# The second feed-forward product by seven products of quarter matrices instead of eight

## The reference

```python
xW = einsum('ntd,dh->nth', x, Wx) + b
next_h = tanh(xw_t + prev_h @ Wh)            # scan over 2048 steps, h0 = cond_1024
...
def quant_linear(x, w, b):
    xq, s_in = quant_act_uint8(x)             # one scale for the whole tensor: max / 255
    wq, s_w = quant_weight_int8_perchannel(w) # one scale per output row: max|w| / 127
    bq = quant_bias_int32(b, s_in, s_w)
    return einsum('btd,fd->btf', xq, wq) + bq
h = relu(quant_linear(rnn, w1, b1))
return x + quant_linear(h, w2, b2)
```

## Time and profile before

| what | value |
|---|---|
| three runs | 501.76, 502.87, 497.11 us |
| span of the profiled execution (first to last instruction) | 496.8 us |
| TensorE busy | 477.3 us, 96% |
| VectorE, ScalarE, GpSimd busy | 293.4, 235.6, 94.8 us |
| mean granted clock of TensorE | 0.997 |
| second product on the chain of waits | from 382.6 us on |
| bytes moved | 65.37 MB |

### The profile page before, as it was taken

How to read it: one execution, slowest core, us unless ns; L and a number is a source line. 1 busy time by engine, 2 the same in 40 slices (tenths; PEclk the granted TensorE clock), 3 DMA queues, 4 the chain that set the end, 5 groups by cost and what they waited for, 6 DMA issues and landing times.

```text
span 496.8 us, 8656 instructions
## 1 busy us (share of the span) xinstructions
PE 477.3 (96%) x3003; PEld 326.9 (66%) x3003; DVE 293.4 (59%) x476; ACT 235.6 (47%) x450; POOL 94.8 (19%) x69
## 2 busy tenths in 40 slices
PE   8989999999999999999767999999999999999997
PEld 3668888888999999999754444444443444444443
DVE  2797664468233354545678978878778433454442
ACT  0324544554333232323573888888884334343340
POOL 2840471210000000000000000000000554444355
PEclk9998999999999999999999999999999999999999
DMA  8974422110349000000000777200002089888883
GB/s 294 386 257 169 171 86 84 41 46 1 74 95 169 0 1 0 0 0 0 2 1 3 299 294 323 101 0 1 0 1 85 35 302 303 304 274 306 308 314 133
DMA packets 38165, 65.37 MB, mean 132 GB/s; under 512 B 19056, under 2 KB 19200, under 8 KB 34560
## 3 DMA queue, kind: packets, MB, share of 16 engines
q1 hardware_dynamic: 37472, 64.04, 37.4%
q10 hardware_dynamic: 576, 1.05, 0.6%
q0 software_dynamic: 96, 0.01, 0.0%
HBM read 39.93 MB, written 20.97 MB: 123 GB/s over the span
## 4 chain that ended last, share of the span: by engine, by line
PE 87%; DVE 7%; DMA 2%; ACT 1%; issue 1%; SPq 1%; DVEq 0%; ACTq 0%
PE bank L794 22%; PE bank L859 22%; PE bank L584 15%; PE bank L621 12%; PE bank L627 12%; PE bank L611 3%; DMA arena<-w 2%; DVE arena L1203 2%; PE bank L647 2%; DVE arena L1342 1%; DVE w_absmax L1196 1%; ACT arena L1059 1%; DVE arena L1562 0%; SPq L424 0%; DVE arena L1252 0%
## 5 line engine op out<-in xcount | busy, mean ns | idle before, releaser
L560 POOL TENSOR_SCALAR arena<-arena,bq 128x512 f32<-128x512 f32 x32 | 53.2, 1676 | 336.9 <-DVEq L1605 284.4
L794 PE MATMUL bank<-arena,w_words 128*128 128x512 f16 (+1 forms) x512 | 110.7, 379 | 0.7 <-DVE arena L1440 0.7
L859 PE MATMUL bank<-arena,w2t 128*128 128x512 f16 x512 | 110.7, 379 | 0.5 <-DVE arena L1568 0.5
L1098 ACT ACTIVATE arena<-bank,bq,s_bits 128x512 f32<-128x512 f32 x124 | 89.1, 774 | 27.3 <-PE bank L794 15.0
L859 PEld LDWEIGHTS bank<-arena,w2t 128*128 128x128 f16 x512 | 49.7, 98 | 61.5 <-DVE arena L1562 2.0
L794 PEld LDWEIGHTS bank<-arena,w_words 128*128 128x128 f16 x512 | 50.0, 98 | 61.0 <-DVE arena L1440 1.5
L1521 DVE TENSOR_REDUCE hid_parts<-arena 128x1 f32<-128x1024 f32 x60 | 72.2, 1216 | 20.4 <-ACT arena L1098 19.8
L621 PE MATMUL bank<-arena 128*128 x512 | 63.5, 277 | 0.1
L627 PE MATMUL bank<-arena 128*128 x512 | 62.4, 275 | 0.0
L621 PEld LDWEIGHTS bank<-arena 128*128 128x128 f32 x512 | 59.7, 192 | 0.7 <-issue 0.5
L627 PEld LDWEIGHTS bank<-arena 128*128 128x128 f32 x512 | 59.7, 192 | 0.0
(11 more groups left out here) (104 smaller groups left out, 354.9 us busy)
## 6 DMA issues: line engine op xcount, KB each, us to landing
spill<-arena SPq DMA_DIRECT2D x12, 1024.0 KB, 3.9
arena<-spill SPq DMA_DIRECT2D x12, 1024.0 KB, 8.4
arena<-w SPq DMA_DIRECT2D x8, 1024.0 KB, 5.2
arena<-x_t SPq DMA_DIRECT2D x32, 256.0 KB, 3.9
y_t<-arena SPq DMA_DIRECT2D x32, 256.0 KB, 2.1
arena<-x_t SPq DMA_DIRECT2D x7, 1024.0 KB, 8.8
arena<-x_t ACTq DMA_DIRECT2D x4, 256.0 KB, 5.7
arena<-wx SPq DMA_DIRECT2D x4, 256.0 KB, 5.4
```

The lines of the kernel that those rows point to most:

```text
L560: nc.gpsimd.tensor_scalar(xb[:, d], xb[:, d], bq2[:, d:d + 1], None, ALU.add).then_inc(xb_ready, 1)
L794: mm = nc.tensor.matmul(bank[:, f % 8, :], w1t[:, k, f * P:(f + 1) * P], states_in[:, k, :], start=(k == 0), stop=(k == KT - 1))
L859: return nc.tensor.matmul(bank[:, 4 + d, :], w2t[:, f, d * P:(d + 1) * P], hq[:, f % HQ_RING, :], start=(f == 0), stop=(f == FT - 1))
L1098: kept = nc.scalar.activation(out[:, e, :], bank[:, (f + e) % 8, :], ACT.Identity, bias=bq1[:, f + e:f + e + 1], scale=s1_bits[:, f + e:f ...
```

## The change

Group 4 goes first and keeps the plain product of 64 matmuls. The other seven follow in the order 0, 1, 2, 3, 5, 6, 7 (`ORDER`). For each of them the hidden values (2048 x 512) and w2 are cut into quarters, and the output's four quarters B00, B01, B10, B11 (halves of the 512 features by halves of the 512 tokens) come from seven products of quarter matrices. A product is 16 matmuls of 256 columns: 8 hidden tiles by 2 output tiles. Products 1, 6, 7 and 4 go into the same bank one upon the other, and between them ScalarE copies the partial result out (`keep_piece`), scaled and with the bias; GpSimd adds the copy to x (`add_piece`); VectorE adds what products 2, 5 and 3 left in the two other banks (`add_out`). VectorE makes four differences of hidden quarters per group (`hidden_sums`, 2048 float16 per partition each), GpSimd three and VectorE one of w2. The hidden integers of a whole group now stand in SBUF, in the first half of the place of their float32 values, two groups ahead.

x and the output lie in memory by groups and quarters, so a partition's part of a group is 8 KB in one piece. The first reload of x is issued right after the spills. The loops over the groups are written out. The waits of the last stage are new.

```diff
+ORDER = (LAST, 0, 1, 2, 3, 5, 6, 7)
+B00, B01, B10, B11 = range(4)
+FIRST_ACT, FIRST_DVE = (1, 3, 5, 7), (0, 2, 4, 6)
+PAIRS_ACT, PAIRS_DVE = (0, 2, 4, 6, 7), (1, 3, 5)
...
-                nc.sync.dma_start(x_in[:, X_ORDER[i]], xT_v[X_ORDER[i]]).then_inc(x_landed[par], 16)
+                nc.sync.dma_start(x_in[:, X_ORDER[i]], x_v[X_ORDER[i]]).then_inc(x_landed[par], 16)
...
             def fetch(s, quarters):
-                sp.wait_ge(relu_ready, (s + 1) * (PAIRS - len(OWN)))
-                sp.wait_ge(own_ready, (s + 1) * len(OWN))
                 for n in quarters:
                     sp.wait_ge(spilled[n], 16 * SPILL)
...
+            def store(n, b):
+                nc.sync.dma_start(y_v[tokens(ORDER[n]), b],
+                                  xb[:, b // 2, b % 2]).then_inc(y_stored[b], 16)
+            def load_again(n, b):
+                if n < GROUPS:
+                    if n > 0:
+                        sp.wait_ge(y_stored[b], 16 * n)
+                    nc.sync.dma_start(xb[:, b // 2, b % 2],
+                                      x_block(ORDER[n], b)).then_inc(xb_landed[b], 16)
+            for b in range(KT):
+                load_again(0, b)
+            sp.wait_ge(hid_act, made_by_act(0, PAIRS))
+            sp.wait_ge(hid_dve, made_by_dve(0, PAIRS))
+            fetch(0, (1, 2))
+            sp.wait_ge(plain_ready, KT)
+            fetch(0, (0, 3))
+            for b in range(KT):
+                sp.wait_ge(piece_added[2 * (b // 2)], 1)
+                sp.wait_ge(piece_added[2 * (b // 2) + 1], 1)
+                store(0, b)
+                if b % 2 == 1:
+                    load_again(1, b - 1)
+                    load_again(1, b)
+            sp.wait_ge(out_ready[B00], 1)
+            store(1, B00)
+            load_again(2, B00)
+            for n in SECOND:                       # 1 to 7
+                if n > 1:
+                    sp.wait_ge(out_ready[B01], n - 1)
+                    store(n - 1, B01)
+                    load_again(n, B01)
+                s = (n - 2) // 2 + 1
+                if s in range(1, SPILL):           # n = 2 to 5
+                    sp.wait_ge(second[3], s)
+                    fetch(s, (2 * (n % 2),))
+                sp.wait_ge(out_ready[B11], n)
+                store(n, B11)
+                load_again(n + 1, B11)
+                if n == GROUPS - 1:
+                    sp.wait_ge(out_ready[B00], n)
+                    store(n, B00)
+                sp.wait_ge(piece_added[B10], n + 1)
+                store(n, B10)
+                load_again(n + 1, B10)
+                if n < GROUPS - 2:
+                    sp.wait_ge(out_ready[B00], n + 1)
+                    store(n + 1, B00)
+                    load_again(n + 2, B00)
+                if s in range(1, SPILL):
+                    fetch(s, (2 * (n % 2) + 1,))
...
+            # GpSimd: three sums of w2 (f16, 128 x 2048), four additions for group 4, then
+            def add_piece(n, b):
+                pool.wait_ge(xb_landed[b], 16 * (n + 1))
+                pool.wait_ge(piece_kept[b], n + 1)
+                nc.gpsimd.tensor_tensor(block, block, piece(b), ALU.add).then_inc(piece_added[b], 1)
+            add_piece(1, B00)
+            for n in SECOND:
+                add_piece(n, B11)
+                if n < GROUPS - 1:
+                    add_piece(n + 1, B00)
+                add_piece(n, B01)
+                add_piece(n, B10)
...
+            # TensorE
+            def quarter_product(m, at, weights, values, first=False):
+                for k in range(HALF_F):            # 8
+                    for j in range(2):
+                        mm = nc.tensor.matmul(bank[:, at, j * HALF:(j + 1) * HALF],
+                                              weights[:, k, j * P:(j + 1) * P], values[:, k, :], ...)
+                mm.then_inc(second[m], 1)
+            def second7(n):
+                pe.wait_ge(w2_sums, 3)
+                pe.wait_ge(hid_sums, sums_made(n, 3))
+                pe.wait_ge(piece_kept[B01], n + 1)
+                quarter_product(7, chain_bank(n), w2_sum(2), hidden_sum(n, 3))
+            def second4(n):
+                pe.wait_ge(hid_sums, sums_made(n, 4))
+                pe.wait_ge(piece_kept[B11], n + 1)
+                ...
+            def second3(n):
+                pe.wait_ge(w2_last_sum, 1)
+                pe.wait_ge(out_ready[B11], n)
+                ...
+            second1(1)
+            second2(1)
+            for n in range(1, GROUPS - 2):
+                second6(n)                         # waits for piece_kept[B00]
+                second1(n + 1)
+                second7(n)
+                second5(n)
+                second4(n)
+                second2(n + 1)
+                second3(n)
+            # n = 6: 6(6) 1(7) 7(6) 5(6) 4(6) 3(6);  n = 7: 6 5 7 2 4 3
...
+            # ScalarE
+            def hidden_pair(n, p):
+                if n > KEPT:
+                    act.wait_ge(fetched[p // 2], 16 * (n - KEPT))
+                ...
+            def keep_piece(n, b, product):
+                act.wait_ge(second[product], n)
+                act.wait_ge(piece_added[b], n)
+                for j in range(2):
+                    kept = nc.scalar.activation(piece(b)[:, j, :], bank[...], ACT.Identity,
+                                                bias=bq2[...], scale=s2_bits[...])
+                kept.then_inc(piece_kept[b], 1)
+            for n in range(1, GROUPS - 1):
+                keep_piece(n, B01, 6)
+                if n == 1:
+                    hidden_pair(2, 6)
+                    hidden_pair(2, 7)
+                keep_piece(n + 1, B00, 1)
+                keep_piece(n, B11, 7)
+                hidden_pair(n + 2, 0)
+                hidden_pair(n + 2, 2)
+                keep_piece(n, B10, 4)
+                hidden_pair(n + 2, 4)
+                hidden_pair(n + 2, 6)
+                hidden_pair(n + 2, 7)
...
+            # VectorE
+            for n in range(1, GROUPS - 1):
+                if n > 1:
+                    add_out(n - 1, B01, CROSS_BANK, 3)
+                hidden_sums(n + 1)                 # four differences
+                add_out(n, B11, CROSS_BANK, 5)
+                hidden_pair(n + 2, 1)
+                hidden_pair(n + 2, 3)
+                if n < GROUPS - 2:
+                    add_out(n + 1, B00, SUM_BANK, 2)
+                hidden_pair(n + 2, 5)
```

More of the change, by code:

```diff
@@ L515, in _ @@
-            store(GROUPS - 2)
-            load_again(GROUPS - 1)
-            store(GROUPS - 1)
-            for d in range(KT):
-                sp.wait_ge(y_stored[d], 16 * GROUPS)
+                    nc.sync.dma_start(part(slot_at(KEPT + 1 + s) + n * quarter, quarter),
+                                      spill[s, :, n * quarter:(n + 1) * quarter]).then_inc(fetched[n], 16)
+            def store(n, b):
+                nc.sync.dma_start(y_v[tokens(ORDER[n]), b],
+                                  xb[:, b // 2, b % 2]).then_inc(y_stored[b], 16)
@@ L522, in _ @@
+            sp.wait_ge(out_ready[B01], GROUPS - 1)
+            store(GROUPS - 1, B01)
+            for b in range(KT):
+                sp.wait_ge(y_stored[b], 16 * GROUPS)
         @block.gpsimd
@@ new lines, in second1, with second2 @@
+            def second1(n):
+                wait_hidden(n, HALF_F // 2 - 1)
+                if n > 2:
+                    pe.wait_ge(piece_kept[B10], n - 1)
+                quarter_product(1, chain_bank(n), w2_part(0, 0), hidden_part(n, 0, 0), first=True)
+            def second2(n):
+                wait_hidden(n, PAIRS - 1)
+                if n > 1:
+                    pe.wait_ge(out_ready[B00], n - 1)
+                quarter_product(2, SUM_BANK, w2_part(1, 0), hidden_part(n, 1, 0), first=True)
@@ L1173, in _, with first_hidden @@
-            relus(LAST, None)
-            with act.Fori(SPILLED[0], GROUPS) as g:
-                relus(g, lambda f: keep[:, g - SPILLED[0], f:f + 2, :],
-                      fetches=g - (SPILLED[0] - 1))
+            def first_hidden(p):
+                f = 2 * p
+                if p >= HALF_F // 2:
+                    act.wait_ge(hid_dve, made_by_dve(0, 0))
+                    act.wait_ge(hid_act, made_by_act(0, 1))
+                if f in HELD:
+                    for e in range(2):
+                        made = nc.scalar.activation(
+                            hidden_ints(0, p)[:, e, :], bank[:, (f + e) % 8, :], ACT.Relu,
+                            bias=bias1[:, f + e:f + e + 1], scale=scale1[:, f + e:f + e + 1])
+                else:
+                    made = nc.scalar.activation(hidden_ints(0, p), last_pair(f), ACT.Relu,
+                                                scale=s_hid_inv[:, 0:1])
+                made.then_inc(hid_act, 1)
@@ new lines, in _ @@
+            first_hidden(1)
+            first_hidden(3)
+            act.wait_ge(scales2_ready, 1)
+            first_hidden(5)
+            act.wait_ge(acc_kept, ACC_RING + GROUPS * PAIRS - len(HELD) // 2)
```

(25 more changed lines are left out.)

413 lines of the change are left out of this document (229 added, 184 removed).

## The result

The changed kernel takes 573.67 us (median of four runs, 571.17 to 575.94), the kernel before beside it 502.18 (497.11 to 502.87): 71.5 us slower, a ratio of 1.146 (95% interval 1.140 to 1.151). Forecast were +22.6 and a range up to 540. The direction was right; the size was wrong threefold.

The account below looks back on a forecast made before the run. TensorE was taken as the bound, with little room at the DMA. Terms -11.3 - 0.3 + 4 + 27.5 + 1 + 1.7 = +22.6 took the span from 496.8 to 519.4; 5.0 more for the median gave 524 us, range 505 to 540.

Parts of the forecast that it names:

- TensorE: Seven groups of the second product at 12.2 us a turn instead of 13.82, at 0.109 a matmul: -11.3 us.
- SyncE's list: Second stage: SyncE waits for each store before its reload, 16.7 us per pass against TensorE's 12.2, delaying P7(6): +27.5 us.
- The opening: Start of the quarter products: first stores and reloads stand behind two 1 MB fetches, so P4(1) comes late: +4 us.
- Work that hides: Written-out loops, group 4's first pair, GpSimd's sums of w2 and the engines' work per turn: no cost, cover gone +1.
- The end: After TensorE's last product: keep, GpSimd addition, store issue and landing end 4.6 us behind it instead of 3.6: +1 us.
- The clock: After one long wait TensorE runs at a granted clock of 0.50 for a while: +1.7 us.
- The queue keeps up: Rival for SyncE's queue: only the last fetch is late, +4.8, 506.6 us; chance 0.20.
- VectorE is the bound: Rival for the turns: VectorE's slow sums or the port shared with GpSimd make its turn 16.1, 534 us; chance 0.17.
- Faster: Rival: the last fetch lands before P7(6) needs it and the opening hides, -6 to -10, 494 us; chance 0.08.
- the -0.3 for the x layout: Loads of x to SBUF get longer pieces, one in the chain that starts the kernel: a gain of 0.3 us.
- the lower end for TensorE: The best end of TensorE's gain, at 0.108 a matmul: -11.8 us.
- the fetch of the faster case: Last fetch in SyncE's pass 5, to be issued by 7.3 us after c5, the start of TensorE's turn 5.

Follow-up runs that it names:

- e14: e13 with the fetches of groups 6 and 7 cut to a sixty-fourth of their bytes: 498.44 us.
- e9: The changed kernel with VectorE instead of GpSimd making the three sums of w2, and two pairs of group 1 converted earlier: 560.66 us.
- e10: Against e9: output apart from x, so reloads wait for no store, and every list in the order in which blocks come ready: 518.20 us.
- e12: Against e10: only B10 and B11 apart from x, B00 and B01 back in x's place, GpSimd adding B11 ahead of B01: 514.59 us.
- e13: Against e12: GpSimd adds B11 ahead of the next group's B00, and the fetches are spread over more passes: 507.04 us, 1.016 times the kernel before.

## Why the prediction was wrong in size

The forecast's span was 519.4, the measured one 572.4: +53.0. By its own steps:

- **TensorE: right.** 0.109 a matmul forecast, 0.109 measured; a turn without waits is 12.5 in e14 against 12.2 forecast and 13.82 before.
- **SyncE's list: right mechanism, mis-sized; +34.4 of the 53.0.** From `second6(2)` to `second7(6)` I had 79.9 us; it took 544.46 - 430.21 = 114.3. The failed term is the landing: 4 x 2.1 + 2 x 2.75 = 13.9 us a pass, measured 22.4 (n = 4). I took 2.1 us from a kernel whose stores had only other stores ahead of them, and had myself written that SyncE issues a reload between two stores. Each store stands behind that reload (3.5), and the two behind a fetch behind both (7.5 to 7.8 instead of 2.1 + 2.75 = 4.85). The four passes took 93.6 instead of 66.8, which is 26.8 of the 34.4; pass 2 began 10.0 us after `second6(2)` (440.19) instead of 4.2, another 5.8; the last fetch landed after 7.4 instead of 5.7. What was foretold of its shape came: waits at `keep_piece`, the longest in turn 6, ScalarE's longest for the spill, SyncE's for its own stores and longest behind a fetch.
- **The opening: wrong, +14.1.** `second6(2)` was due at 399.9 + 12.2 + 4 = 416.1 and came at 430.2. Here the failed step is that GpSimd's three sums stand under "Work that hides" and cost nothing. I sized them a little high (5.5; measured 4.05 to 4.50) and asked when they were due, but not what they keep from VectorE while they run. The row that would have told was in the forecast, under a rival: a conversion and an addition that met took 2.17 and 2.13 in place of 1.23 and 1.37. Scale and first conversion came 5.2 us later by this, the stages before it 2.5 (e9, e10, e12 to e14 start the plain products at 380.0 to 381.6, so that part isn't the change's). The plain products then took 406.05 - 390.33 = 15.7 instead of 13.8, the first of them at a granted clock of 0.56. The remaining 4.5 are mostly VectorE's list: sums of 1.22 took 2.2 to 2.3 beside GpSimd's additions and held up the conversions for `second1(2)`, for which TensorE stood 5.23.
- **The end: +2.7.** TensorE ended at 565.1 and the span 7.3 later, forecast 4.6: GpSimd's last but one addition stood 3.99 us for a reload (GpSimd's timeline):

```profile
566.07 1.26 POOL L680 TENSOR_TENSOR arena<-arena,w_words 128x512 f32<-128x512 f32 x1 [3.99 <-DMA arena<-x_t]
```

- **The clock.** 27 matmuls took 5.87 us after the wait of 22.3, 0.217 each, at 0.50, the lower level of 1.2 GHz: 2.9 us lost instead of 1.7, and TensorE needed 20.6 from there to its end instead of 17.4 + 1.7: +1.5. The other long waits cost it too, but behind SyncE's list.
- **The rivals.** *The queue keeps up* fell with passes of 23.4 on average. *VectorE is the bound* was wrong for the turns (its sums took 1.35 us on average, with 1.6 taken) and right in its reason, the shared port, for the opening, where I had not put it. The Trainium skill, "VectorE: DVE Perf Modes", section "The perf-mode tier table (the rule you actually need)", has 1224 ns for such a sum; the trace agrees where GpSimd is idle, with 1.22. *Faster* is the rival that e13 and e14 speak to: with every list reordered the kernel is 1.6% slower, and without the bytes of two groups level. There TensorE's turns save 1.3 us each, and the opening, with `second6(2)` at 419.0 in e14 where TensorE's work alone would allow 380.2 + 13.8 + 3.5 + 12.2 = 409.7, gives them back.

The range ended at 540 because both ends of the pass came from stores that follow no reload. With 3.5 and 7.5 the same sum would have been 519.4 + 4 x (22.0 - 13.9) = 552, and 14 more with the opening. Of the smaller terms, the -0.3 for the x layout is shown by no run. Three slips in the working change little: the DMA shares are those of stretches of 15.5 and 14.0 us, so that a group of 13.82 has 11.2 to 12.3 us of DMA; the lower end for TensorE is -12.1, not -11.8; and the fetch of the faster case would have to be issued by c5 + 6.8, not 7.3.

Left open: whether a better opening would bring e13 below the kernel before, which was not tried, and how much of e10's step each single order is worth.

## What to carry to other kernels

Before you put "wait for the store, then reload" into one engine's list, write down what stands ahead of each transfer in its queue in the new order, and price the landing from rows with the same predecessor. For work put on an idle engine, ask not only when it is due but who can't run while it does; between GpSimd and VectorE that was whole instructions here (3.38 and 3.97 us for work of 0.17). A stage that is tight on one resource (0.8 to 0.9 of the DMA here) leaves little to win on another: shorter turns must carry the same bytes.

## What was unexpected of the hardware

- A VectorE product of 128 x 8 numbers took 3.38 and 3.97 us (0.17 alone) while GpSimd ran two-input sums of 4.05 us; reductions of one input beside the same sums took 0.22 to 0.28, as always.
- A 256 KB store landed after 2.1 us behind other stores only (the median before), 3.5 behind a 256 KB reload, 7.5 to 7.8 behind a reload and a 1 MB fetch (n = 4), and 7.6 beside four fetches of another queue.
- One wait of TensorE near 35 us, in code that no experiment touched, was 0.0 to 5.0 us long and moved single runs by as much.
